# Attention layer 0 of a four-layer gated model: the softmax denominator split between GpSimd and the vector engine, and TensorE's filler products taken out

## The chip, the cores and the metric

The kernel runs on one NeuronCore of one Trainium2 chip. The core has TensorE (PE in the profile), the vector engine (DVE), the scalar engine (ACT), GpSimd (POOL) and SyncE (SP, which here only issues DMAs). The metric is the device time of one execution in microseconds (us); lower is better.

## The reference, cut to what matters

`x` is 16 batches of 256 rows of 128 numbers; the context has 64 rows a batch. Four layers follow each other, each a gated cross attention and a gated feed-forward. Only the attention of layer 0 is touched. Its softmax is unusual: it runs over the heads (axis 1), not over the keys.

```python
Q, K, V = query @ Wq.T + bq, key @ Wk.T + bk, value @ Wv.T + bv      # 16 heads of 8
energy = einsum('bhqd,bhkd->bhqk', Qh, Kh) / sqrt(8)
attn = softmax(energy, axis=1)                                       # over the 16 heads
out = einsum('bhqk,bhkd->bhqd', attn, Vh)
x = x + tanh(g_xattn[0]) * (out @ Wo.T + bo)
```

## The kernel before, in words

One program on five engines; each engine executes its own list in order, and semaphores hold the order between them. Each `Stage` field (`q.sub`, `q.esc`, `q.prob` and so on) is a semaphore with its base, and `q.sub(n)` means "n of these are done".

In attention layer 0 the 4096 rows of x are 32 tiles of 128 queries. A **unit** u is one tile; two units, an even one (qt = 0) and an odd one (qt = 1), are one batch b = u // 2, a **pair**. The scores of a unit are 128 partitions x 1024 numbers, ordered (head, key). They pass through these steps:

- PE `scores(b)` (L545) computes both units of a batch into the four banks of `psS`, at the end of even unit 2b - 4. It waits for DVE to have read the batch before (`q.sub(2 * b)`), for the queries, and for `kblk(b)`, the keys spread by head, which POOL writes in `keys` (L730).
- DVE `score_rows(u)` takes the maximum over heads (L672) and subtracts it into one of four slots of `sp`, a part of the tile `ring` (L676).
- ACT `exp_rows(u)` takes the exponential in place (L634).
- DVE `sum_rows(u)` adds up the 16 heads for each key (L688, read with a step of 64 numbers) and inverts the sum into `rden` (L690).
- POOL `scale(u)` multiplies the slot by the inverse, in place (L750). This is `prob(u)`.
- PE turns the slot in two halves h = 0, 1 of four 128 x 128 transposes (L554) through the one bank `psT`; ACT copies each half to `pT` (L638); PE multiplies by the values (L563) into `psO`; DVE copies the result (L694, `output`); PE projects it (L593) and adds the bias row (L594); DVE adds it to x (L699, `residual`); DVE then takes the statistics of the new rows for the next norm (L375).

The work is staggered. In its unit u an engine does:

- DVE: `score_rows(u+3)`, `output(u-1)`, `residual(u-2)`, `sum_rows(u+2)`, statistics of u-2.
- POOL: if u is even `keys(b+2)`, if u is odd `values(b+1)` (L739), then `scale(u+2)`.
- ACT: the copy of half 0; if u is even the queries, keys and values of batch b+2; the copy of half 1; `exp_rows(u+3)`.
- PE: transposes of u half 0; if u is even the projections of batch b+2 (L520 to L526); values of u-1, half 0; transposes of u half 1; values of u-1, half 1; projection of u-2; if u is even `scores(b+2)`.

PE also executes products that nothing reads (`keep_clock`, L533): four of the identity by itself ahead of each `scores` from batch 2 on, after the wait for `q.sub`, and three ahead of the first transposes of each unit from 1 on, after the wait for `q.pT`. Each such float32 product is two matmul records in the profile. The tile `late` is not in use in this stage, except that SP's zeroing DMAs read its part `zeros`, `late[:, 2 * CT:3 * CT]`.

Of the kernel before, what the change touches and what calls it, by code (L numbers as in the profile page):

```python
# [12 lines left out]
ALU = mybir.AluOpType  # L13
# [8 lines left out]
P = 128  # L22
B, S, SK, D = 16, 256, 64, 128
NH, DK = 16, 8
NT = B * S // P
CH = 4
NC = NT // CH
CT = CH * P
# [38 lines left out]
class Stage:  # L67


    def __init__(self, std=None, xn=None, xt=None, xnT=None, xs=None, kept=None, xa=None, ctx=None, kraw=None, vraw=None, kv=None, qp=None, qT=None, kblk=None, vblk=None, scores=None, mx=None, sub=None,  # L70
# [16 lines left out]
RN_STEPS = 13  # L87
LN_STEPS = dict(std=1, xn=NC, xa=NC, xt=NC, xnT=NC)
LN_PLACE = {0: 0, 1: 1}
ATT_STEPS = dict(kraw=B, vraw=B, kv=B, qp=B, qT=B, kblk=B, vblk=B, scores=B, mx=NT, sub=NT, esc=NT, esum=NT, erec=NT, prob=NT,  # L90
                 t=2 * NT, pT=2 * NT, o=NT, attnT=NT, y=NT, x=NT)
FFN_NAMES = "up act y x dup dact dy copied xgt xgT ye ix"

# [1 line left out]
def build(nc, ins, out, sorted_x, sorted_y):  # L95
    ctx = ExitStack()
    with ctx:
# [13 lines left out]
        ident = sb("ident", [P, P])  # L111
# [43 lines left out]
        kblk = sb("kblk", [P, 2, GH, SK])  # L155
        vblk = sb("vblk", [P, 2, NP, 4 * DK])
        ring = sb("ring", [P, NS, NH * SK])
        sbs, sp = ring[:, 0:2], ring[:, 2:6]
        pT = sb("pT", [P, 2, NP, P])
        mx = sb("mx", [P, 4, SK])  # L160
        kraw = sb("kraw", [P, 2, SK])
        vraw = sb("vraw", [P, 2, D])
# [7 lines left out]
        late = sb("late", [P, 5 * CT])  # L170
        xstage = late[:, 0:2 * CT].rearrange("p (s t d) -> p s t d", s=2, t=CH)
        zeros = late[:, 2 * CT:3 * CT]
        b2copy = late[:, 3 * CT:5 * CT].rearrange("p (s t d) -> p s t d", s=2, t=CH)
        wtn = b2copy[:, 0, 0:2]
        xg = sbs[:, 0, :].rearrange("p (s n) -> p s n", s=2)
# [16 lines left out]
        rows = sb("rows", [P, NT * 2], I32)  # L192
# [30 lines left out]
        psT = pb("psT")  # L223
# [288 lines left out]
        def known(k, low, high=NT + 2):  # L512

            return k is None or low <= k < high

        def att_tensor(pe, l):
            q = AT[l]

            def queries(b):
                nc.tensor.matmul(psM[:, 0:S], wat[:, l, 0, :], xnT[:, bass.ds(b * S, S)], start=True, stop=True).then_inc(q.qp.sem, 1)  # L520

            def keys_values(b, s):
                nc.tensor.matmul(psM[:, S:S + SK], wat[:, l, 1, :], ctxz[:, bass.ds(b * 2 * SK + SK, SK)], start=True, stop=True)
                for h in range(2):
                    at = S + SK + h * D // 2
                    mm = nc.tensor.matmul(psM[:, at:at + D // 2], ctxz[:, b * 2 * SK + (1 - h) * SK:b * 2 * SK + (3 - h) * SK],  # L526
                                          wat[:, l, 2, h * D // 2:(h + 1) * D // 2], start=True, stop=True)
                mm.then_inc(q.kv.sem, 1)

            def keep_clock(bank, count):  # L530

                for _ in range(count):
                    nc.tensor.matmul(bank, ident[:], ident[:], start=True, stop=True)  # L533

            def scores(b, s, first):
                if not first:
                    pe.wait_ge(*q.sub(2 * b))
                if not isinstance(b, int) or b > 1:
                    keep_clock(psS[:, 0, 0:P], 4)
                pe.wait_ge(*q.qT(b + 1))  # L540
                pe.wait_ge(*q.kblk(b + 1))
                for g in range(NG):
                    r = slice(32 * g, 32 * g + 32)
                    for qt in range(QT):
                        mm = nc.tensor.matmul(psS[:, g, qt * 256:qt * 256 + 256], qTs[r, s, qt * P:(qt + 1) * P],  # L545
                                              kblk[r, s, :, :].rearrange("p h k -> p (h k)"), start=True, stop=True)
                mm.then_inc(q.scores.sem, 1)

            def transpose_rows(u, j, h, first):
                if not first:  # L550
                    pe.wait_ge(*q.pT(2 * u + h))
                for i in range(4):
                    p = 4 * h + i
                    mm = nc.tensor.transpose(psT[:, i * P:(i + 1) * P], sp[:, j, p * P:(p + 1) * P], ident[:])  # L554
                mm.then_inc(q.t.sem, 1)

            def times_values(u, s, qt, h):

                pe.wait_ge(*q.pT(2 * u + h + 1))
                for g in (2 * h, 2 * h + 1):  # L560
                    for pp in range(2):
                        a = 2 * g + pp
                        mm = nc.tensor.matmul(psO[32 * g:32 * g + 32, qt, 0:P], vblk[:, s, a, :], pT[:, qt, a, :],  # L563
                                              start=(pp == 0), stop=(pp == 1), tile_position=(0, 32 * g))
                if h:
                    mm.then_inc(q.o.sem, 1)

            def unit(u, b, s, qt, k):
                j = 2 * s + qt
                last_s = s if qt else 1 - s  # L570
                if known(k, 1, NT):
                    pe.wait_ge(*q.pT(2 * u))
                    keep_clock(psT[:, 0:P], 3)
                if known(k, 0, NT):
                    pe.wait_ge(*q.prob(u + 1))
                    transpose_rows(u, j, 0, k == 0)
                if qt == 0 and known(k, 0, NT - 2 * QT):
                    pe.wait_ge(*q.vraw(b + 2))
                    pe.wait_ge(*q.qT(b + 2))
                    keys_values(b + 2, s)  # L580
                    queries(b + 2)
                if known(k, 1, NT + 1):
                    if known(k, 3):
                        pe.wait_ge(*q.x(u - 2))
                    pe.wait_ge(*q.vblk(b + qt))
                    times_values(u - 1, last_s, 1 - qt, 0)
                if known(k, 0, NT):
                    transpose_rows(u, j, 1, False)
                if known(k, 1, NT + 1):
                    times_values(u - 1, last_s, 1 - qt, 1)  # L590
                if known(k, 2):
                    pe.wait_ge(*q.attnT(u - 1))
                    nc.tensor.matmul(psO[:, qt, 256:256 + D], attnT[:, qt, :], wat[:, l, 3, :], start=True, stop=False)  # L593
                    nc.tensor.matmul(psO[:, qt, 256:256 + D], ones1[:, :], bo[:, l, :], start=False, stop=True).then_inc(q.y.sem, 1)  # L594
                if qt == 0 and known(k, 0, NT - 2 * QT):
                    scores(b + 2, s, False)

            def first_queries():
                pe.wait_ge(*LN[2 * l].xnT(1))
                pe.wait_ge(*q.vraw(2))  # L600
                queries(0)
                pe.wait_ge(*q.qT(1))
                queries(1)


            pe.wait_ge(s_vz, 1)
            if l == 0:
                pe.wait_ge(ld["attw"], 9 * 16)
            keys_values(0, 0)
            pe.wait_ge(*q.vraw(1))  # L610
            keys_values(1, 1)
            ln_tensor(pe, 2 * l, None, first_queries, lambda: scores(0, 0, True))
            pe.wait_ge(*LN[2 * l].xnT(NC))
            scores(1, 1, False)
            for k in range(NT + 2):
                unit(k, k // QT, k // QT % 2, k % QT, k)
# [48 lines left out]
        def att_vector(dve, l):  # L665
# [14 lines left out]

            def sum_rows(u, j, early):

                dve.wait_ge(*q.esc(u + 1))
                if not early:
                    dve.wait_ge(*q.prob(u - 1))
                rd = rden[:, j % 2, :]
                rows = sp[:, j, :].rearrange("p (h k) -> p k h", k=SK)
                nc.vector.tensor_reduce(rd, rows, AXX, ALU.add).then_inc(q.esum.sem, 1)  # L688
                dve.wait_ge(*q.esum(u + 1))
                nc.vector.reciprocal(rd, rd).then_inc(q.erec.sem, 1)  # L690
# [31 lines left out]
        def att_gpsimd(pool, l):  # L722
# [10 lines left out]
            def values(b, s, early):  # L733
# [8 lines left out]
                        bvh[:, :].rearrange("k (h g e d) -> k g h e d", h=2, g=NG, e=2)[:, :, :, pp, :], ALU.add)  # L742
                op.then_inc(q.vblk.sem, 1)

            def scale(u, j):

                buf = sp[:, j, :].rearrange("p (h k) -> p h k", k=SK)
                rd = rden[:, j % 2, :].rearrange("p (a k) -> p a k", a=1)
                pool.wait_ge(*q.erec(u + 1))
                nc.gpsimd.tensor_tensor(buf, buf, rd.broadcast_to([P, NH, SK]), ALU.mult).then_inc(q.prob.sem, 1)  # L750

            def unit(u, b, s, qt, k):
                j = 2 * s + qt
                if qt == 0 and known(k, 0, NT - 2 * QT):
                    keys(b + 2, s, False)
                if qt == 1 and known(k, 0, NT - QT):
                    values(b + 1, 1 - s, not known(k, 2))
                if known(k, 0, NT - 2):
                    scale(u + 2, (j + 2) % 4)

            for b in range(2):
                keys(b, b, True)
            values(0, 0, True)
            for v in range(1, 3):
                scale(v - 1, v - 1)
            units(pool, unit, 0)


# [1238 lines left out]
```

## Time and profile before

| | us |
|---|---|
| median of 3 runs | 1236.53 |
| lowest and highest | 1236.52, 1237.42 |
| the profiled execution | 1235.94 |
| its span in the profile | 1233.8 |
| attention layer 0 in it, first score reduce to last residual | 45.4 to 242.8 |

In rows of a timeline the first number is the start in us from the span's start, the second the duration; a bracket gives idle time just before the instruction and what ended it. Rows of groups give count, busy time, mean ns of one, and idle time before them. "PEclk" is the granted clock of TensorE as a share of its full 2.4 GHz, so that 0.50 is 1.2 GHz.

### The profile page before, as it was taken

The numbers are of one execution on the slowest core, as the hardware profiler recorded it, in microseconds if no ns is written. First come the engines' busy times: TensorE is split into PE (matmuls) and PEld (weight loads), VectorE is DVE, ScalarE is ACT, GpSimd is POOL, SyncE is SP. The second block draws the span as 40 slices with busy tenths as digits, with TensorE's granted clock in tenths as the row PEclk, the third lists the DMA queues.
The fourth block names the chain that finished last, engine by engine and source line by source line (L and its number), as shares of the span: only waits on it lengthen the run. The fifth ranks groups of instructions, "written<-read, shape, count | busy, mean of one in ns | idle before, by whom it ended". The sixth has DMA issues, their size and how long they took to land.

```text
span 1233.8 us, 25957 instructions
## 1 busy us (share of the span) xinstructions
PE 1022.7 (83%) x9008; PEld 827.8 (67%) x9008; DVE 783.6 (64%) x1696; ACT 633.9 (51%) x1462; POOL 611.6 (50%) x660
## 2 busy tenths in 40 slices
PE   1599999762999899994877989999999998739990
PEld 0477767552677899982556767677777776539990
DVE  2889899726204766863889978645545667746661
ACT  1544444331323566664665787666555656426660
POOL 0145554312777303708886776744454547465224
PEclk9899999955999899997999999999999999859995
DMA  8920000000111123311000000000050000013224
GB/s 247 286 63 1 1 1 1 1 0 9 48 64 52 53 75 88 108 46 31 20 21 8 2 1 2 2 2 1 2 154 1 1 2 2 1 54 93 83 71 111
DMA packets 75475, 55.80 MB, mean 45 GB/s; under 512 B 7411, under 2 KB 68467, under 8 KB 75252
## 3 DMA queue, kind: packets, MB, share of 16 engines
q1 hardware_dynamic: 69236, 41.92, 11.8%
q0 software_dynamic: 6144, 12.60, 3.4%
q8 instruction: 61, 1.00, 0.3%
q14 instruction: 34, 0.28, 0.1%
HBM read 32.48 MB, written 22.02 MB: 44 GB/s over the span
## 4 chain that ended last, share of the span: by engine, by line
PE 65%; DVE 15%; issue 7%; ACT 5%; POOL 4%; SPq 1%; DMA 1%; DVEq 1%; POOLq 0%; ACTq 0%
PE psS L1052 8%; PE psT L1499 6%; PE psO L1058 5%; PE psO L1563 5%; PE psS L1555 4%; PE psS L1488 3%; PE psO L1514 3%; PE psS L1058 3%; PE psO L981 3%; PE psS L973 3%; DVE rden L688 2%; POOL xrows L1210 2%; DVE x L1123 2%; PE psO L1521 2%; DVE ring L676 2%
## 5 line engine op out<-in xcount | busy, mean ns | idle before, releaser
L1828 POOL TENSOR_TENSOR ring<-ring,mx 128x1024 f32<-128x1024 f32 x96 | 182.2, 1905 | 121.3 <-DVE mx L1724 120.7
L1631 ACT ACTIVATE pT<-psT 128x512 f32<-128x512 f32 x192 | 114.4, 596 | 147.4 <-PE psT L1499 147.3
L1101 ACT ACTIVATE pT<-psS,b1copy 128x128 f32<-128x128 f32 x512 | 145.9, 368 | 84.7 <-PE psS L1052 84.6
L1210 POOL DMA_INDIRECT xrows<-sorted_y,rows x96 | 93.3, 971 | 184.9 <-DMA sorted_y<-pT 132.7
L1052 PE MATMUL psS<-ring 128*128 128x128 f32 x1024 | 138.7, 280 | 10.4 <-DVE ring L1141 9.7
L1716 DVE TENSOR_TENSOR ring<-psS,bias 128x1024 f32<-128x1024 f32 x96 | 113.0, 1219 | 44.6 <-PE psS L1488 44.1
L1499 PE MATMUL psT<-ident,ring 128*128 128x128 f32 x768 | 123.0, 284 | 17.0 <-ACT pT L1631 10.3
L1052 PEld LDWEIGHTS psS<-ring 128*128 128x128 f32 x1024 | 126.9, 195 | 12.5 <-DVE ring L1141 6.7
L750 POOL TENSOR_TENSOR ring<-ring,rden 128x1024 f32<-128x1024 f32 x32 | 75.4, 2355 | 115.3 <-DVE rden L690 115.3
L1499 PEld LDWEIGHTS psT<-ident,ring 128*128 128x128 f32 x768 | 86.8, 143 | 57.4 <-issue 34.5
L1724 DVE TENSOR_REDUCE mx<-ring 128x16 f32<-128x1024 f32 x96 | 112.1, 1209 | 0.0
L1138 DVE COPY ring<-w 128x512 f32 x128 | 59.8, 467 | 58.7 <-PE psO L1058 23.1
L1058 PE MATMUL psO<-ring,pT 128*128 128x128 f32 x640 | 86.0, 278 | 0.4 <-ACT pT L1101 0.3
L1058 PEld LDWEIGHTS psO<-ring,pT 128*128 128x128 f32 x640 | 79.1, 195 | 0.7 <-ACT pT L1101 0.7
L638 ACT ACTIVATE pT<-psT 128x512 f32<-128x512 f32 x64 | 38.2, 597 | 75.2 <-PE psT L554 75.2
L1243 POOL DMA_INDIRECT sorted_x<-late,ix x64 | 62.4, 975 | 23.4 <-issue 16.8
L1662 ACT ACTIVATE xn<-x,lnb,lnr 128x128 f32<-128x128 f32 x160 | 65.7, 492 | 11.8 <-POOL lnb L1849 11.8
L1769 DVE TENSOR_TENSOR x<-psO,x 128x512 f32<-128x512 f32 x16 | 11.1, 692 | 88.0 <-PE psO L1563 88.0
L688 DVE TENSOR_REDUCE rden<-ring 128x64 f32<-128x1024 f32 x32 | 61.4, 1919 | 0.0
L1563 PE MATMUL psO<-w,xrows 128*128 128x128 f32 x512 | 59.9, 276 | 0.3 <-ACT vblk L1653 0.3
L1563 PEld LDWEIGHTS psO<-w,xrows 128*128 128x128 f32 x512 | 58.4, 192 | 0.5 <-issue 0.5
L1007 ACT ACTIVATE ring<-psS,b 128x512 f32<-128x512 f32 x32 | 22.0, 687 | 69.4 <-PE psS L973 69.2
(273 smaller groups left out, 2251.9 us busy)
## 6 DMA issues: line engine op xcount, KB each, us to landing
w<-w_dram SPq DMA_DIRECT2D x34, 256.0 KB, 6.0
ring<-sorted_x SPq DMA_DIRECT2D x32, 256.0 KB, 2.9
sorted_y<-pT SPq DMA_DIRECT2D x32, 256.0 KB, 2.5
sorted_x<-late SPq DMA_DIRECT2D x20, 256.0 KB, 3.6
xrows<-sorted_y,rows POOLq DMA_INDIRECT x96
ctxz<-ctxz_dram SPq DMA_DIRECT2D x1, 1056.0 KB, 11.6
wat<-wat_dram SPq DMA_DIRECT2D x4, 256.0 KB
w<-w_dram SPq DMA_DIRECT2D x8, 128.0 KB, 2.6
```

Of the source, the lines that this page charges most:

```text
L688: nc.vector.tensor_reduce(rd, rows, AXX, ALU.add).then_inc(q.esum.sem, 1)
L750: nc.gpsimd.tensor_tensor(buf, buf, rd.broadcast_to([P, NH, SK]), ALU.mult).then_inc(q.prob.sem, 1)
L1052: mm = nc.tensor.matmul(psS[:, t % 2, f * P:(f + 1) * P], wcopy[:, t, 0, f, :], xgT[:, s, t * P:(t + 1) * P], start=True, stop=True)
L1058: mm = nc.tensor.matmul(moe_out[r][:, s, t * P:(t + 1) * P], hs[:, t % 2, f, :], wcopy[:, t, 1, f, :], start=(f == 0), stop=(f == nf - 1))
L1101: op = nc.scalar.activation(hs[:, t % 2, f, :], psS[:, t % 2, f * P:(f + 1) * P], func, bias=b1copy[:, t, f:f + 1])
L1210: nc.gpsimd.indirect_dma_start(fetched[:, at + m, :], None, sorted_y[c // (NC // 2)], bass.IndirectOffsetOnAxis(rows[:, c * nt + m:c * nt ...
L1499: mm = nc.tensor.transpose(psT[:, i * P:(i + 1) * P], ring[:, u % NS, p * P:(p + 1) * P], ident[:])
L1563: mm = nc.tensor.matmul(psB[:, t * P:(t + 1) * P], fourT[:, i % 2, k, t * P:(t + 1) * P], w22[:, e, f, :], start=(k == 0), stop=(k == 3))
L1631: nc.scalar.activation(pT[:, u % 2, 4 * h:4 * h + 4, :].rearrange("p a q -> p (a q)"), psT[:, :], ACT.Exp).then_inc(s_pT, 1)
L1716: nc.vector.tensor_tensor(ring[:, u % NS, :].rearrange("p (g h k) -> p g h k", g=NG, h=GH), psS[:, :, qt * 256:(qt + 1) * 256].rearrange(" ...
L1724: nc.vector.tensor_reduce(mx[:, u % 4, 0:NH], ring[:, u % NS, :].rearrange("p (h k) -> p h k", k=SK), AXX, ALU.max).then_inc(s_max, 1)
L1828: nc.gpsimd.tensor_tensor(rows_, rows_, mx[:, u % 4, 0:NH].rearrange("p h -> p h ()").broadcast_to([P, NH, SK]), ALU.subtract).then_inc(s_ ...
```

## The change

`late[:, 0:2 * CT]` gets a second name, `hsum`, with two slots of 512 numbers. POOL's new `add_halves(u)` waits for the exponentials of u and adds heads 8 to 15 of the slot to heads 0 to 7 into `hsum` (128 x 512). DVE's `sum_rows(u)` waits for that (`q.added`) in place of the exponentials and reduces 8 partial sums for each key in place of 16. In POOL's unit u `add_halves(u+3)` stands after `scale(u+2)`. `keep_clock` and both calls of it go.

```diff
+        hsum = late[:, 0:2 * CT].rearrange("p (s n) -> p s n", s=2)
...
-            def keep_clock(bank, count):
-
-                for _ in range(count):
-                    nc.tensor.matmul(bank, ident[:], ident[:], start=True, stop=True)
-
             def scores(b, s, first):
                 if not first:
                     pe.wait_ge(*q.sub(2 * b))
-                if not isinstance(b, int) or b > 1:
-                    keep_clock(psS[:, 0, 0:P], 4)
...
                 if known(k, 1, NT):
                     pe.wait_ge(*q.pT(2 * u))
-                    keep_clock(psT[:, 0:P], 3)
...
             def sum_rows(u, j, early):
 
-                dve.wait_ge(*q.esc(u + 1))
+                dve.wait_ge(*q.added(u + 1))
...
-                rows = sp[:, j, :].rearrange("p (h k) -> p k h", k=SK)
+                rows = hsum[:, j % 2, :].rearrange("p (h k) -> p k h", k=SK)
...
+            def add_halves(u, j, early):
+
+                pool.wait_ge(*q.esc(u + 1))
+                if not early:
+                    pool.wait_ge(*q.esum(u - 1))
+                half = NH * SK // 2
+                nc.gpsimd.tensor_tensor(hsum[:, j % 2, :], sp[:, j, 0:half], sp[:, j, half:], ALU.add).then_inc(q.added.sem, 1)
+
...
                 if known(k, 0, NT - 2):
                     scale(u + 2, (j + 2) % 4)
+                if known(k, 0, NT - 3):
+                    add_halves(u + 3, (j + 3) % 4, False)
...
-            for v in range(1, 3):
-                scale(v - 1, v - 1)
+            add_halves(0, 0, True)
+            add_halves(1, 1, True)
+            scale(0, 0)
+            add_halves(2, 2, False)
+            scale(1, 1)
             units(pool, unit, 0)
```

## Rows read from the trace of the kernel before

**Rows 1.** Stretches of 10 us: PE, PEld, DVE, ACT, POOL busy, then PEclk, DMA

```profile
50.00:60.00 10.00, 6.36 (x33) 4.94 (x33) 9.86 (x10) 4.27 (x8) 4.79 (x3) 0.50 1.03 295
...
100.00:110.00 10.00, 9.30 (x83) 7.04 (x83) 9.06 (x12) 4.71 (x8) 4.66 (x5) 1.00 0.01 2
```

**Rows 2.** DVE's timeline over one pair and a little more

```profile
108.03 1.91 DVE L688 TENSOR_REDUCE rden<-ring 128x64 f32<-128x1024 f32 x1
...
109.98 0.55 DVE L690 RECIPROCAL rden<-rden 128x64 f32<-128x64 f32 x1
...
110.60 1.20 DVE L672 TENSOR_REDUCE mx<-psS 128x64 f32<-128x1024 f32 x1
...
111.94 1.23 DVE L676 TENSOR_TENSOR ring<-psS,mx 128x1024 f32<-128x1024 f32 x1
...
114.16 0.35 DVE L699 SCALAR_TENSOR_TENSOR x<-psO,tg,x 128x128 f32 x1 [0.63 <-PE psO L594]
...
114.43 1.93 DVE L688 TENSOR_REDUCE rden<-ring 128x64 f32<-128x1024 f32 x1
...
119.95 1.92 DVE L688 TENSOR_REDUCE rden<-ring 128x64 f32<-128x1024 f32 x1
```

**Rows 3.** The timeline of PE, ACT and POOL over the same pair

```profile
107.72 1.16 PE L533 MATMUL psS<-ident 128*128 128x128 f32 x8 [0.65 <-DVE ring L676]
...
108.81 1.17 PE L545 MATMUL psS<-kblk,qTs 32*128 32x256 f32 x16
...
109.90 0.94 PE L533 MATMUL psT<-ident 128*128 128x128 f32 x6
...
110.61 2.37 POOL L750 TENSOR_TENSOR ring<-ring,rden 128x1024 f32<-128x1024 f32 x1 [2.47 <-DVE rden L690]
...
110.67 0.60 PE L554 MATMUL psT<-ident,ring 128*128 128x128 f32 x4
...
113.53 0.48 PE L594 MATMUL psO<-bo,ones 1*128 1x128 f32 x2
...
114.72 0.60 PE L554 MATMUL psT<-ident,ring 128*128 128x128 f32 x4
...
118.49 0.48 PE L594 MATMUL psO<-bo,ones 1*128 1x128 f32 x2
```

**Rows 4.** Groups by line, operation and shape, whole span

```profile
L750 POOL TENSOR_TENSOR ring<-ring,rden 128x1024 f32<-128x1024 f32 x32 | 75.4, 2355 | 115.3 <-DVE rden L690 115.3
...
L1855 POOL TENSOR_TENSOR x<-x,bx 128x512 f32<-128x512 f32 x24 | 30.5, 1270 | 0.0
...
L1828 POOL TENSOR_TENSOR ring<-ring,mx 128x1024 f32<-128x1024 f32 x96 | 182.2, 1905 | 121.3 <-DVE mx L1724 120.7
...
L730 POOL TENSOR_TENSOR kblk<-kraw,hmask 128x256 f32<-128x256 f32 x16 | 11.6, 725 | 24.5 <-ACT kraw L627 24.5
...
L1724 DVE TENSOR_REDUCE mx<-ring 128x16 f32<-128x1024 f32 x96 | 112.1, 1209 | 0.0
```

**Rows 5.** PE's timeline in a later stage, at its longer idle times

```profile
603.41 0.66 PE L1499 MATMUL psT<-ident,ring 128*128 128x128 f32 x4 [2.02 <-POOL ring L1828]
...
612.22 0.69 PE L1514 MATMUL psO<-pT,late 128*32 128x128 f32 x16 [2.60 <-DVE vraw L1733]
...
612.85 2.09 PE L1488 MATMUL psS<-xnT,qTs 32*128 32x256 f32 x16
...
614.87 1.11 PE L1499 MATMUL psT<-ident,ring 128*128 128x128 f32 x4
```

**Rows 6.** Stretches of 2 us of that stage: PE busy, PEclk, DMA

```profile
612.00:614.00 2.00, 1.78 (x28) 0.67 0.00 0
...
616.00:618.00 2.00, 2.00 (x26) 0.98 0.13 33
```

**Rows 7.** DVE's sums at the two ends of the stage

```profile
72.33 1.92 DVE L688 TENSOR_REDUCE rden<-ring 128x64 f32<-128x1024 f32 x1
...
227.04 1.92 DVE L688 TENSOR_REDUCE rden<-ring 128x64 f32<-128x1024 f32 x1
```

More of the change, by code:

```diff
@@ L89 @@
 LN_PLACE = {0: 0, 1: 1}
-ATT_STEPS = dict(kraw=B, vraw=B, kv=B, qp=B, qT=B, kblk=B, vblk=B, scores=B, mx=NT, sub=NT, esc=NT, esum=NT, erec=NT, prob=NT,
+ATT_STEPS = dict(kraw=B, vraw=B, kv=B, qp=B, qT=B, kblk=B, vblk=B, scores=B, mx=NT, sub=NT, esc=NT, added=NT, esum=NT, erec=NT, prob=NT,
                  t=2 * NT, pT=2 * NT, o=NT, attnT=NT, y=NT, x=NT)
```

## The prediction

> **What bounds the kernel now.** I read the stretches of 10 us first. While attention layer 0 is in full swing, DVE is busy for 9.06 of 10 us and PE for 9.30, GpSimd for 4.66 and ACT for 4.71, at full clock; the stage starts at half clock, 0.50 [rows 1]. Two engines look full, so the shares don't decide. PE's share is partly the products that nothing reads: in one pair 8 records ahead of `scores` and 6 ahead of each unit's first transposes [rows 3].
>
> Second, DVE's timeline. I measure by the starts of its sums, two for a pair: 108.03 (in an even unit), 114.43 (odd), 119.95 (even) [rows 2]. So the even half of a pair lasts 6.40 us, the odd half 5.52, a pair 11.92. In the odd half DVE never idles: sum, reciprocal, maximum and subtraction alone take 1.92 + 0.55 + 1.20 + 1.23 = 4.90 us of 5.52 and the rest are the small copies. In the even half it idles 0.63 us ahead of the residual, released by PE's bias product [rows 2].
>
> Third, what PE did until then. Released by DVE's subtraction at 107.72, it ran the products that nothing reads (1.09 us to the next start), the scores (1.09), products again (0.77), then from the first transposes at 110.67 to the bias product at 113.53, which ends 0.48 later [rows 3]. So in the even half the path is DVE subtraction, PE, DVE residual, and 1.86 us of it is filler. In the odd half it is DVE. GpSimd waits 2.47 us for the reciprocal before its scale [rows 3] and bounds nothing.
>
> **The change, part by part.** In what follows 0 is the start of the sum in an even unit, u + 2.
>
> *The sum of half the numbers.* The trace has no reduce of 512 strided numbers. The strided one of 1024 takes 1.92 us [rows 2]; a contiguous one of 1024 takes 1.21 [rows 4]. From below 0.60, half of the contiguous one; from above 1.13, half of 1.92 plus half of the 0.35 that 128 numbers cost at L699 [rows 2], as if all of that were a fixed part. I take 1.04, near the upper end, since the step of 64 numbers stays. To the start of the reciprocal that is 1.07. The Trainium skill (VectorE: DVE Perf Modes, The perf-mode tier table) has every `tensor_reduce` at one element a cycle, which would give an estimate of 0.69 for 512; our row of 1.92 for 1024 contradicts it for this access, and by 0.69 a pair would be 0.35 shorter.
>
> *GpSimd's new addition*, 128 x 512, two inputs. L1855 is an addition of that size: 1.27 us [rows 4]. Below: 0.95, half of L1828 (1.905); above: 1.35, half of L750 (2.355) plus the 0.17 that I allow for a fixed part. I take 1.27. The Trainium skill (GPSIMD Reference, Engine selection) speaks against this edit: elementwise work of two inputs belongs on VectorE, GpSimd being about twice as slow. In busy time it is right here: 1.27 us are bought to save 0.88 on DVE. But GpSimd had 2.47 us idle, so what counts is whether it lies in a loop.
>
> *It does lie in one, and that is the new wait.* GpSimd's order is scale(u+2), addition(u+3); DVE's is sum(u+3), reciprocal. The sum waits for the addition, the addition is queued behind the scale, the scale waits for the reciprocal before. One turn: sum 1.07, reciprocal to scale 0.63 (109.98 to 110.61), scale 2.35, addition 1.27, handoff 0.08 (as from the reciprocal's end at 110.53 to 110.61) [rows 2 to 4]. Sum: **5.40 us**. DVE alone would need 5.52 - 0.88 = 4.64, so it now waits some 0.7 us ahead of the sum; behind the waiting sum stand the reciprocal, the statistics and the next maximum. The odd half is 5.40 instead of 5.52: of DVE's 0.88, only 0.12 is left.
>
> *The keys are pushed back too.* `keys(b+2)` is queued behind addition(u+2), so it starts at -0.08, takes 0.73 [rows 4], and PE's `scores(b+2)` can't start before 0.71, though DVE freed the bank about a microsecond earlier. From there: scores 1.09, first transposes to residual 3.49 (110.67 to 114.16), residual to sum 0.27 [rows 2, 3]; no filler. Even half: 0.71 + 1.09 + 3.49 + 0.27 = **5.56 us** (GpSimd's loop would allow 5.40), against 6.40. The scores end at about 1.9, DVE wants them at 1.69, a wait of 0.3 that this path hides.
>
> A pair is then 5.40 + 5.56 = **10.96 us** against 11.92. From the sum at 72.33 to the one at 227.04 are 13 pairs [rows 7], 154.7 us; 13 x 10.96 = 142.5. That is 12.2 us less. At the start the extra work of GpSimd and the lost filler meet the cold clock in both versions; I count nothing, with 3 us either way. At the end the last scale waits for one more turn of 5.40 where DVE did it in 3.6; filler ahead of the last transposes goes; 0.3 us more. So far **-11.9 us**.
>
> *What the filler hid.* Without it PE has, in my schedule, this in each pair: scores at 0.71, odd unit's transposes at 1.80, its bias product at 4.66, even unit's transposes at 5.08 (0.42 behind it; the scale that they need ended at 4.05), end of its bias product 4.25 later (114.72 to 118.97) at 9.33 [rows 3]. Then it is idle until the scores at 10.96 + 0.71 = 11.67: **2.34 us**, once a pair, where it had 0.65. The trace shows what such gaps do. In the later attention stage PE idled 2.02 us until 603.41 and kept the full clock; it idled 2.60 us until 612.22 and then had half clock (0.67 on average from 612 to 614), with full clock again from about 616 [rows 5, 6]. They are the nearest below and above; 2.34 is in the middle. Half clock cost there 2.09 us for scores that take 1.17 at full clock [rows 3] and 1.11 for transposes that take 0.66: 0.92 + 0.45 = 1.37 us, and in the even half the scores and transposes are on the path. I take the clock to fall in 6 of the 13 pairs: 6 x 1.37 = 8.2 us. It can't stay low: PE's 8.3 us of work in a pair would be over 14 at half clock, more than the pair, so PE would be busy throughout, as it was in the stretch ahead of the rise at 616 [rows 6].
>
> Sum: -11.9 + 8.2 = **-3.7 us**. The profiled execution took 1235.94 (span 1233.8 and 2.1 around it), the median of the runs is 1236.53, 0.6 more; -3.7 from the median is 1232.8.
>
> **The rivals.**
>
> *The clock holds* in all pairs. For it: the gap of 2.02 was harmless, and if the true sum or addition is cheaper the gap shrinks with it. Then all of the 11.9 stays: 1236.5 - 11.9 = 1224.6.
>
> *The clock falls in every pair*, the other side. Place: the scores and transposes behind the 2.34 us gap. Price 1.37 x 13 = 17.8, less 11.9: 5.9 us slower, 1242.4; and more where a fall lasts longer than there. It decides from 8.7 falls on (11.9 / 1.37). For it: the gap of 2.60 cost the clock, and every shift that makes GpSimd later widens the gap. Against it: the gap comes at the same place of each pair, but the odds that I read from two rows are even, not certain.
>
> *The shorter sum isn't shorter*, so that the change doesn't do what it says: if the 1.92 came from something other than the count, the odd half is 5.40 + 0.88 = 6.28, the even one still 5.56 (DVE has room there), a pair 11.84. That saves 1 us, and the gap grows to 3.2, longer than the one that cost the clock: 1236.5 - 1 + 17.8 = 1253. Against it: a contiguous reduce of the same 1024 numbers takes 1.21, so most of it goes by the elements.
>
> *The sum and addition are cheaper than I take* (0.60 and 0.95): the odd half would be 4.6 to 4.7, a pair near 10.2, the gap 1.6, no falls: 13 x 1.7 = 22 us, 1214. Both at their lower ends is unlikely.
>
> **How the numbers follow.** Falls on some pairs, 1232.8 with 1228 to 1238 around it: 0.42. Clock holds: 0.26. Falls in every pair: 0.22. Sum not shorter, or another wait: 0.06. Both prices at their ends: 0.04. For 8 in 10 the range runs from 1222 (clock holds, and a little of the start) to 1244 (falls everywhere, one or two of them long). A measurement of this kernel tells a change from none at about 0.2%, 2.5 us. Faster by more: 0.28 of the first case, 0.25, 0.04, together 0.57 and 0.02 of the rest: 0.59. Within: 0.12 of the first, 0.05 of the others: 0.17. Slower: 0.24.
>
> **What the profile of the changed kernel would show.** Sums of half the size near 1.04 us, additions near 1.27; DVE idle ahead of the sum, released by GpSimd, about 0.7 us in odd halves; PE idle ahead of the scores near 2.3 us once a pair, released by GpSimd's keys; sums 5.56 and 5.40 us apart in pairs at full clock, and half clock in some of the pairs. If PEclk is 1.00 from 70 us to 240, the forecast is too high by 8. If pairs are longer than 11.9 it is too low. It would be wrong otherwise if the addition slowed ACT or DVE beside it, or if the later stages' clock falls at other places because all of them come earlier.

## The result, and the profile after

| | before | after |
|---|---|---|
| median, us | 1236.53 (4 runs) | 1259.16 (4 runs) |
| lowest and highest | 1235.46, 1237.42 | 1252.46, 1262.70 |
| the profiled execution, and its span | 1235.94, 1233.8 | 1262.70, 1260.9 |
| mean granted clock in it | 0.927 | 0.884 |
| attention layer 0, last residual ends at | 242.8 | 265.3 |

The change makes the kernel slower: ratio 1.0172, 95% interval 1.0148 to 1.0195, 22.6 us in the medians. That is above the forecast of 1232.8 and above its range of 1222 to 1244. In the profiled executions, of which that of after is the slowest of its four, the spans differ by 27.1 us. Of these, 22.5 lie in the stage that was edited: its last residual ends that much later. What follows took 995.6 us against 991.0. That part has no edit in any kernel here and took 989.5 to 995.0 in the first group of runs below, so I don't put its 4.6 us down to the change.

I read the page of after first: busy time by engine, and the granted clock in 40 slices.

```profile
PE 1031.6 (82%) x8710; PEld 822.5 (65%) x8710; DVE 756.4 (60%) x1696; ACT 634.2 (50%) x1462; POOL 652.5 (52%) x692
...
PEclk9787777755699899998899999999999999868995
```

The clock shows 7 and 8 in the slices from 60 to 250 us. In stretches of 10 us, the same columns as [rows 1], the full clock of before is gone there:

```profile
100.00:110.00 10.00, 9.35 (x68) 6.32 (x64) 7.31 (x11) 4.38 (x9) 5.84 (x6) 0.79 0.00 1
110.00:120.00 10.00, 8.38 (x55) 5.96 (x56) 5.82 (x9) 3.60 (x5) 5.61 (x6) 0.66 0.01 2
120.00:130.00 10.00, 7.72 (x57) 5.09 (x57) 7.83 (x12) 3.10 (x6) 8.11 (x7) 0.74 0.00 0
```

DVE, busy for 9.06 of 10 us in [rows 1], is down to 5.82 to 7.83: it has less to do and waits more. Now one pair in the timeline (start, duration, engine; the bracket is idle time and what ended it), to be set beside [rows 2, 3]:

```profile
123.16 1.27 POOL L744 TENSOR_TENSOR late<-ring 128x512 f32<-128x512 f32 x1
124.39 0.72 POOL L723 TENSOR_TENSOR kblk<-kraw,hmask 128x256 f32<-128x256 f32 x1
124.46 1.03 DVE L681 TENSOR_REDUCE rden<-late 128x64 f32<-128x512 f32 x1 [0.60 <-POOL late L744]
125.25 2.11 PE L539 MATMUL psS<-kblk,qTs 32*128 32x256 f32 x16 [2.28 <-POOL kblk L723]
126.15 2.35 POOL L751 TENSOR_TENSOR ring<-ring,rden 128x1024 f32<-128x1024 f32 x1 [1.04 <-DVE rden L683]
127.30 1.11 PE L548 MATMUL psT<-ident,ring 128*128 128x128 f32 x4
128.34 1.08 PE L557 MATMUL psO<-pT,vblk 128*32 128x128 f32 x8
129.35 1.12 PE L548 MATMUL psT<-ident,ring 128*128 128x128 f32 x4
130.39 1.08 PE L557 MATMUL psO<-pT,vblk 128*32 128x128 f32 x8
132.52 0.35 DVE L692 SCALAR_TENSOR_TENSOR x<-psO,tg,x 128x128 f32 x1 [0.70 <-PE psO L587]
132.79 1.02 DVE L681 TENSOR_REDUCE rden<-late 128x64 f32<-128x512 f32 x1
138.18 1.03 DVE L681 TENSOR_REDUCE rden<-late 128x64 f32<-128x512 f32 x1 [0.69 <-POOL late L744]
```

The order is the forecast one: addition (L744), then keys (L723), then PE's scores (L539) after an idle 2.28 us that the keys end. But everything PE then does takes the time of half clock: scores 2.11 us, transposes 1.11, values products 1.08, transposes 1.12, values products 1.08. The sums are at 124.46, 132.79 and 138.18: the even half lasts 8.33 us where 5.56 was forecast, the odd half 5.39 (5.40 forecast). PE and PEclk in stretches of 2 us around that gap:

```profile
122.00:124.00 2.00, 0.98 (x8) 1.00 0.00 0
124.00:126.00 2.00, 0.75 (x8) 0.69 0.00 0
126.00:128.00 2.00, 2.00 (x20) 0.50 0.00 0
128.00:130.00 2.00, 2.00 (x13) 0.50 0.00 0
130.00:132.00 2.00, 2.00 (x14) 0.60 0.00 0
132.00:134.00 2.00, 2.00 (x15) 1.00 0.00 0
```

The 0.69 from 124 to 126 puts the fall to 1.2 GHz at 124.76, half a microsecond before the gap ends; the 0.60 from 130 to 132 puts the rise at about 131.6. So 6.8 us at half clock, and the stretch from 132 on is at 2.4 GHz again.

I placed every fall in this way, from stretches of 1 us. Between the sum of tile 4 (72.61) and that of tile 30 (247.32) the clock falls 13 times, once in each pair. The first two low spells last 3.4 us, and their even halves 7.00 and 6.91; the other eleven last 6.8 us (one fall every 13.65 us) and go with even halves of 8.23 to 8.34. In this pattern pair and clock fit each other: an even half of 8.3 with an odd one of 5.35 is a pair of 13.65 us, just the distance between two falls, so each pair meets the fall at the same place. Behind these pairs, in the stage's tail, the clock falls once more, at 247.63 us, and stays low for 13.65 us. In before it holds to the end of the stage, until 244.0. The tail of after, same columns as above:

```profile
248.00:261.00 13.00, 12.88 (x68) 8.25 (x67) 4.38 (x11) 3.17 (x6) 6.47 (x5) 0.50 0.00 1
```

The groups of the edited lines, whole span:

```profile
L744 POOL TENSOR_TENSOR late<-ring 128x512 f32<-128x512 f32 x32 | 40.7, 1271 | 24.4 <-ACT ring L627 24.4
L681 DVE TENSOR_REDUCE rden<-late 128x64 f32<-128x512 f32 x32 | 32.9, 1029 | 10.6 <-POOL late L744 10.6
L539 PE MATMUL psS<-kblk,qTs 32*128 32x256 f32 x256 | 31.9, 632 | 35.0 <-POOL kblk L723 30.8 <-issue 4.2
```

Addition 1271 ns and sum 1029 ns are the prices of the forecast (1.27 and 1.04). The scores waited 30.8 us in all for the keys.

### The profile page after: what moved, and what is told of

It reads as the page before. It is cut to its first block, busy times and chain, and to the rows that moved or that the text cites. A ratio compares the mean times of both kernels' runs of the same rounds, so it can differ in the third digit from the quotient of the medians.

```text
span 1260.9 us, 25429 instructions
## 1 busy us (share of the span) xinstructions
PE 1031.6 (82%) x8710; PEld 822.5 (65%) x8710; DVE 756.4 (60%) x1696; ACT 634.2 (50%) x1462; POOL 652.5 (52%) x692
## 4 chain that ended last, share of the span: by engine, by line
PE 60%; issue 15%; DVE 9%; POOL 8%; ACT 4%; SPq 1%; DMA 1%; DVEq 1%; POOLq 0%; ACTq 0%
PE psS L1058 9%; PE psT L1505 6%; PE psO L1064 5%; PE psO L1569 5%; PE psS L1561 4%; PE psO L1520 3%; PE psS L1494 3%; PE psS L1064 3%; PE psO L987 3%; POOL late L744 3%; PE psS L979 3%; DVE x L1129 2%; POOL xrows L1216 2%; PE psO L1527 2%; PE psO L1460 2%
## 5 line engine op out<-in xcount | busy, mean ns | idle before, releaser
L1834 POOL TENSOR_TENSOR ring<-ring,mx 128x1024 f32<-128x1024 f32 x96 | 182.4, 1907 | 120.0 <-DVE mx L1730 119.5
L1505 PE MATMUL psT<-ident,ring 128*128 128x128 f32 x768 | 124.8, 286 | 19.4 <-ACT pT L1637 11.9
L1668 ACT ACTIVATE xn<-x,lnb,lnr 128x128 f32<-128x128 f32 x160 | 65.8, 494 | 13.8 <-POOL lnb L1855 13.8
L548 PE MATMUL psT<-ident,ring 128*128 128x128 f32 x256 | 57.2, 363 | 4.4 <-POOL ring L751 2.6
L539 PE MATMUL psS<-kblk,qTs 32*128 32x256 f32 x256 | 31.9, 632 | 35.0 <-POOL kblk L723 30.8
```

Source lines behind the costliest of these rows:

```text
L1505: mm = nc.tensor.transpose(psT[:, i * P:(i + 1) * P], ring[:, u % NS, p * P:(p + 1) * P], ident[:])
L1668: op = nc.scalar.activation(to[:, t, :], x[:, c * CH + t, :], ACT.Identity, bias=lnb[:, k, t:t + 1], scale=lnr[:, k, t:t + 1])
L1834: nc.gpsimd.tensor_tensor(rows_, rows_, mx[:, u % 4, 0:NH].rearrange("p h -> p h ()").broadcast_to([P, NH, SK]), ALU.subtract).then_inc(s_ ...
```

## The experiments

Each edit is against the kernel after, if nothing else is said. "Falls" are falls of the clock in the 13 pairs between the sums of tiles 4 and 30; "idle" is PE's idle time from the end of a pair's other work to its scores. Each ratio is to before, from runs on the same chip (kernels of one group share them). The "tail" runs from the sum of tile 30 to the end of the last residual.

### First group: which part of the change costs the time (before: 1238.07)

**e1, both sets of filler products back**, so that only the split of the sum is left.

```diff
+                if not isinstance(b, int) or b > 1:
+                    keep_clock(psS[:, 0, 0:P], 4)
...
                     pe.wait_ge(*q.pT(2 * u))
+                    keep_clock(psT[:, 0:P], 3)
```

> The changed kernel with both sets of filler products back, so that only the split of the sum is left. Clock theory (the loss comes from half clock behind a 2.3 us gap of PE in each pair): the gap is filled to under 1.3 us, PEclk is 1.00 from 70 to 240 us, the even half is 5.56 + 0.77 of filler ahead of the transposes = 6.33, the odd half 5.40, a pair 11.73 against 11.92 of before: about 1234, 2.5 below before. Wait theory (the addition in GpSimd's loop and the late keys are themselves what costs): pairs stay at 13 us or more, 1250 to 1260.

1234.88 us, ratio 0.9966 [0.9953, 0.9979]. Even halves 6.33 to 6.43, odd ones 5.32 to 5.43, no fall, as expected. The split by itself gains 3.2 us: the odd half goes by GpSimd's loop and the even half by PE with its fillers, as the forecast's own terms have it.

**e2, before without its filler products**: the other half of the change alone.

```diff
-                if not isinstance(b, int) or b > 1:
-                    keep_clock(psS[:, 0, 0:P], 4)
...
-                    keep_clock(psT[:, 0:P], 3)
```

> The kernel before with both sets of filler products taken out and nothing else. Clock theory: at full clock the pair would be DVE's own 11.3 us, PE has 8.3 us of work in it and so a gap near 2.7 ahead of the scores, longer than the 2.6 that cost the clock; half clock then adds to the even half what it added in the changed kernel (2.8) less the 1.2 that DVE has in hand: pairs near 12.9, 1245 to 1250. Wait theory: nothing waits longer and 1.86 us of filler leave the path in each pair, DVE's idle 0.63 goes: 13 x 0.63 = 8 us faster, 1228.

1240.95 us, ratio 1.0027 [1.0007, 1.0047]. The idle ahead of the scores is 1.54 and 1.83 us in the first two pairs; there the clock holds and the even halves are 5.42 and 5.51, so the filler really was on PE's path. Behind them the idle is 1.91 to 1.96, and from 95.6 us on the clock falls, 11 times. Nine of the low spells last 3.4 us, with even halves of 6.44 to 6.57; the two of 6.8 us go with 7.8. Around the gap that ends at 118.07:

```profile
116.00:118.00 2.00, 0.15 (x2) 1.00 0.00 0
118.00:120.00 2.00, 1.93 (x22) 0.87 0.00 0
120.00:122.00 2.00, 2.00 (x13) 0.50 0.00 0
122.00:124.00 2.00, 2.00 (x15) 0.78 0.00 0
```

The clock is still full when the scores start and falls at 119.5, behind them. The place of the fall matters little here: the one at 129.7, inside the gap that ends at 130.05, goes with an even half of 6.56, this one with 6.48. A short spell costs 1.0 to 1.1 us here and 1.4 in e3 and e7. A likely reason, argued and not tested, is that the scores start 0.25 us behind DVE's sum here (118.07 and 117.82) and 0.79 behind it in after, so PE has some time in hand. 1240.95 is below the 1245 to 1250 expected. The miss is the price: I had given every fall the 2.8 us of after's long spells, less 1.2.

**e3, only the four products ahead of the scores back.** The first two added lines of e1.

> The changed kernel with only the four filler products ahead of the scores back. They stand in the gap and off the path. Clock theory: gap pieces of 0.7 and 0.6 us, PEclk 1.00, pair 5.56 + 5.40 = 10.96, 1224.6 and so 12 below before. Wait theory: as the changed kernel, 1250 to 1260.

1227.96 us, ratio 0.9899 [0.9865, 0.9933]. The idle is 0.48 ahead of the products and 0.65 behind them. Even halves 5.62 to 5.71, and 7.02 to 7.09 in three pairs: there the clock fell, which I had not expected. The saving is 10.1 us where 12 was expected.

**e4, only the three products ahead of the transposes back.** The last added line of e1.

> The changed kernel with only the three filler products ahead of each unit's first transposes back. Clock theory: they delay PE by 0.77 in the odd unit and 0.77 in the even one, so that the gap ahead of the scores is 2.34 - 0.77 = 1.57 us, shorter than the 2.02 that kept the clock; PEclk 1.00, even half 6.33, odd 5.40, pair 11.73, 1234 to 1235. Wait theory: 1250 to 1260.

1249.86 us, ratio 1.0080 [1.0053, 1.0108]. A miss: I expected the clock to hold. The gap is 1.56 to 1.57 us, below the 2.02 that had been harmless in [rows 5] (1.25 and 1.47 in the first two pairs), and the clock fell 9 times, for 3.4 us each. PE's scores in one pair, and PE with PEclk around them:

```profile
124.08 1.48 PE L544 MATMUL psS<-kblk,qTs 32*128 32x256 f32 x16 [1.57 <-POOL kblk L729]
```

```profile
122.00:124.00 2.00, 0.51 (x3) 1.00 0.00 0
124.00:126.00 2.00, 1.92 (x18) 0.70 0.00 0
126.00:128.00 2.00, 2.00 (x12) 0.50 0.03 8
```

So in these pairs filler products as such don't keep the clock; those in the gap keep it better. e3 and e4 differ in where the products stand, and by 21.9 us. Not all of that is the clock: the three products ahead of the transposes are also on PE's path, and even halves without a fall are 6.33 to 6.43 here and 5.62 to 5.71 in e3, some 9 us in 13 pairs.

### Second group: the size of the gap, and GpSimd's loop (before: 1341.86)

In this group the whole program, before included, took some 100 us more, outside this stage; so I compare within the group and by the halves of the pairs, which were as in the first group. A ratio here stands for about 8% more us than in the other groups.

**e5, six products ahead of the scores.** As e3, with 6 for 4.

> The changed kernel with six filler products ahead of the scores, where the run with four still lost the clock in 3 pairs. Six take 1.65 us of the 2.28 that PE has to wait for the keys and end when the keys do. Clock theory: no or one fall from 70 to 240 us, pairs of 11.05 as in the full-clock pairs with four, 2 to 4 us below the run with four, about 1225. Rival (the falls with four were no matter of idle time, but came of themselves): again 3 or 4 falls, the same time as with four.

1328.02 us, ratio 0.9912 [0.9886, 0.9939]. PE and GpSimd in one pair:

```profile
124.68 1.60 PE L534 MATMUL psS<-ident 128*128 128x128 f32 x12 [0.48 <-DVE ring L676]
125.62 0.73 POOL L730 TENSOR_TENSOR kblk<-kraw,hmask 128x256 f32<-128x256 f32 x1
125.78 1.03 DVE L688 TENSOR_REDUCE rden<-late 128x64 f32<-128x512 f32 x1 [0.70 <-POOL late L751]
126.50 1.17 PE L546 MATMUL psS<-kblk,qTs 32*128 32x256 f32 x16 [0.21 <-POOL kblk L730]
127.60 0.66 PE L555 MATMUL psT<-ident,ring 128*128 128x128 f32 x4
```

The products, 1.60 us of them, end before the keys do and cost nothing: the scores still wait 0.21 for the keys, then take 1.17, not 2.11. No fall in the pairs; even halves 5.62 to 5.72, odd ones 5.32 to 5.43, a pair 11.04. It is 13.8 us below before in the medians. This is the forecast's schedule at full clock (5.56, 5.40, 10.96), and it is 2.6 us a pair shorter than after, with the same work and six products more.

**e6, three small products more, ahead of the wait for the subtraction.**

```diff
+                if not isinstance(b, int) or b > 1:
+                    pe.wait_ge(*q.vraw(b + 1))
+                    for _ in range(3):
+                        nc.tensor.matmul(psM[:, S + SK + D:512], ident[:], ident[:, 0:64], start=True, stop=True)
                 if not first:
                     pe.wait_ge(*q.sub(2 * b))
+                if not isinstance(b, int) or b > 1:
+                    keep_clock(psS[:, 0, 0:P], 6)
```

> As the one with six, and three more products of 64 columns ahead of the wait for the subtraction, in the other piece of the gap (about 0.7 us), into a part of a bank that nothing reads. Clock theory: idle time of PE under 0.5 us a pair, no falls; 1224.6, the time of the rival in which the clock holds. If they make PE late for the scores, the even halves grow by up to 0.3: then 1226 to 1229.

1329.83 us, ratio 0.9916 [0.9893, 0.9940]. The same halves as e5, but for a first even one of 5.87, and no fall. PE idles for less than 0.1 us at a time ahead of the scores; against the 0.48 and 0.21 of e5 that gains nothing more.

**e7, two products ahead of the scores.**

> The changed kernel with two filler products ahead of the scores. PE idles 1.7 us a pair in pieces of 0.7 and 1.1 us, where 2.28 lost the clock in each pair, 1.57 in one piece in 10 of 14, and 1.2 in two pieces in 3. Clock theory (idle time in all counts): falls in 6 to 10 pairs, 1238 to 1248. Rival (only the longest single gap counts): a longest gap of 1.1 is as with four, 2 to 4 falls, 1228.

1337.34 us, ratio 0.9976 [0.9957, 0.9995]. Idle 0.48 and 1.10. Seven falls, each with 3.4 us of half clock, the last of them behind the last scores; even halves 5.62 to 5.71 without one and 6.95 to 7.10 with one, so a fall costs 1.4 us. The count fits "idle time in all" (6 to 10 expected) and not the rival (2 to 4). But the longest single piece also grew, from 0.65 in e3 to 1.10, so a rule by the longest piece is not excluded. The time, 4.5 us below before, is better than the 1238 to 1248 expected. One of the falls:

```profile
118.05 1.33 PE L546 MATMUL psS<-kblk,qTs 32*128 32x256 f32 x16 [1.10 <-POOL kblk L730]
119.31 1.11 PE L555 MATMUL psT<-ident,ring 128*128 128x128 f32 x4
```

```profile
118.00:120.00 2.00, 1.95 (x19) 0.73 0.00 0
120.00:122.00 2.00, 2.00 (x13) 0.50 0.00 0
122.00:124.00 2.00, 2.00 (x17) 0.91 0.00 0
```

**e8, both fillers, no addition**: the sum reads heads 0 to 7 alone, and heads 8 to 15 are left out of the denominator.

```diff
-                dve.wait_ge(*q.added(u + 1))
+                dve.wait_ge(*q.esc(u + 1))
...
-                rows = hsum[:, j % 2, :].rearrange("p (h k) -> p k h", k=SK)
+                rows = sp[:, j, 0:NH * SK // 2].rearrange("p (h k) -> p k h", k=SK)
...
-                    add_halves(u + 3, (j + 3) % 4, False)
```

> Both sets of filler products as before, DVE sums only heads 0 to 7 and heads 8 to 15 are left out of the denominator, GpSimd adds nothing. Against the run with both fillers it takes GpSimd's addition out of the loop and lets the keys go early. Theory (the addition took back DVE's 0.88): the odd half is 5.52 - 0.88 = 4.64, but the even half stays at 6.40 since its path runs through PE, and PE with its fillers has 11.3 us of work in a pair: pairs of 11.3, 1229 to 1230. Rival (DVE's sum is not what set the odd half): 1234, as with the addition.

1329.91 us, ratio 0.9926 [0.9900, 0.9951]. Sums in DVE's timeline:

```profile
118.39 1.03 DVE L689 TENSOR_REDUCE rden<-ring 128x64 f32<-128x512 f32 x1
...
124.62 1.03 DVE L689 TENSOR_REDUCE rden<-ring 128x64 f32<-128x512 f32 x1
...
129.33 0.35 DVE L700 SCALAR_TENSOR_TENSOR x<-psO,tg,x 128x128 f32 x1 [0.26 <-PE psO L595]
129.60 1.03 DVE L689 TENSOR_REDUCE rden<-ring 128x64 f32<-128x512 f32 x1
```

Even half 6.23, odd half 4.98. With the same fillers e1 has 6.33 to 6.43 and 5.32 to 5.43, so GpSimd's addition costs 0.35 to 0.45 in the odd half: that is the loop. An odd half of 4.64 was expected, DVE's own time. It is longer because DVE now waits 0.26 us for PE's bias product in the odd half too. The even half hardly moves (6.20 to 6.30, where 6.40 was expected); PE has it.

### Third group: the keys off GpSimd (before: 1238.32)

**e9, the vector engine spreads the keys, four products ahead of the scores.** GpSimd's `keys` for batches 2 on goes to DVE, ahead of its sum.

```diff
+            def keys(b, s):
+
+                dve.wait_ge(*q.kraw(b + 1))
+                dve.wait_ge(*q.scores(b - 1))
+                nc.vector.tensor_tensor(kblk[:, s, :, :], kraw[:, s, :].rearrange("p (a k) -> p a k", a=1).broadcast_to([P, GH, SK]),
+                                        hmask[:, :, :], ALU.mult).then_inc(q.kblk.sem, 1)
...
                     residual(u - 2, qt)
+                if qt == 0 and known(k, 0, NT - 2 * QT):
+                    keys(b + 2, s)
...
-                if qt == 0 and known(k, 0, NT - 2 * QT):
-                    keys(b + 2, s, False)
```

> The changed kernel with four filler products ahead of the scores, and the spreading of the keys by head moved from GpSimd to the vector engine, ahead of its wait for the sum, where it idles 0.6 us in each pair. Theory (with the clock held, the even half of 5.66 us is keys, scores and PE's products, and the odd half of 5.37 is GpSimd's loop): the scores start 0.8 us earlier, both halves are GpSimd's loop, 5.36, a pair 10.72 against 11.05: 3 to 5 us below the run with six products, 16 below before. Rival (the even half is set by something else): pairs of 11.05 as there, 12 to 14 below before.

1223.88 us, ratio 0.9885 [0.9863, 0.9908]: 14.4 us below before, the lowest ratio of all (16 below was expected; its interval meets those of e3, e5 and e11). Three engines in one pair:

```profile
119.99 1.05 DVE L688 TENSOR_REDUCE rden<-late 128x64 f32<-128x512 f32 x1
124.01 1.27 POOL L760 TENSOR_TENSOR late<-ring 128x512 f32<-128x512 f32 x1
124.32 1.16 PE L534 MATMUL psS<-ident 128*128 128x128 f32 x8 [0.67 <-DVE ring L676]
124.64 0.93 DVE L696 TENSOR_TENSOR kblk<-kraw,hmask 128x256 f32<-128x256 f32 x1
125.49 1.02 DVE L688 TENSOR_REDUCE rden<-late 128x64 f32<-128x512 f32 x1
125.72 1.17 PE L546 MATMUL psS<-kblk,qTs 32*128 32x256 f32 x16 [0.24 <-DVE kblk L696]
130.88 1.04 DVE L688 TENSOR_REDUCE rden<-late 128x64 f32<-128x512 f32 x1 [0.17 <-POOL late L760]
```

Idle 0.67 and 0.24. The even half is 5.39 (125.49 to 130.88), now GpSimd's loop, which ends DVE's wait of 0.17; the odd half is 5.50 and DVE's again, since the spread takes 0.93 us there, more than the wait of 0.6 that it was to fill: a pair is 10.83, not the 10.72 expected. Full clock until 211 us, behind the last scores.

**e10, the same with no filler at all.**

> As the one before, without any filler products. Clock theory: PE still has only 8.3 us of work in a pair of 10.7, a gap near 2.1 us ahead of the scores, and loses the clock in each pair; the early keys leave PE's path 0.7 us in hand, so a fall costs 0.7 (if it lasts 3.4 us) to 2.0 (6.8 us): between 6 below and 10 above before. Rival (the late keys were the harm, not the missing products): pairs of 10.7, 15 below before.

1240.52 us, ratio 1.0023 [1.0006, 1.0040]. The gap is 1.68 and 1.77 us in the first two pairs and 1.87 to 1.89 in the others, ended by DVE's keys. The clock falls 13 times, 11 of them for 3.4 us, with even halves of 6.31 to 6.54, and two for 6.8 us, with 7.7 and 7.8. One gap and the scores behind it:

```profile
121.92 2.11 PE L539 MATMUL psS<-kblk,qTs 32*128 32x256 f32 x16 [1.87 <-DVE kblk L689]
```

The same schedule as e9's but for the four products and the clock, and 16.6 us longer.

**e11, the same with six products.**

> Vector engine's keys with six filler products. Theory: six end 0.55 us later than four and push the scores back by that, PE's path is then as long as GpSimd's loop, 5.4; no falls at all, where four may leave one or two: the same time as with four within 3 us.

1226.18 us, ratio 0.9904 [0.9882, 0.9925]. Halves as in e9: four are enough. Its tail takes 19.9 us and e9's 17.3.

**e12, before with only its four products ahead of the scores.**

```diff
                     pe.wait_ge(*q.pT(2 * u))
-                    keep_clock(psT[:, 0:P], 3)
```

> The kernel before with only the four products ahead of the scores; the three ahead of each unit's transposes are out. Clock theory: at full clock the pair would be DVE's own 11.3 us; PE's gap ahead of the subtraction is 1.9 us, as in the run without any, and it loses the clock in most pairs, at a cost of about 1 us each which the shorter path gives back: within 3 us of before. Rival: 8 us below before.

1239.48 us, ratio 1.0013 [0.9999, 1.0027]. Even halves 5.63 to 5.68 at full clock, 7.01 to 7.24 in six pairs with a fall. The gap is 0.68 and 1.27 us in the first two pairs and 1.35 to 1.38 in the others, not the 1.9 expected, and lies ahead of the products. So in before the three products do keep the clock, by ending PE's work later, and what they cost and what they save is about the same.

### All of them by the idle time

| PE idle ahead of the scores, us a pair, from the third pair on | kernel | falls in the 13 pairs |
|---|---|---|
| 0.1 or less | e6, e8 | 0 |
| 0.48 to 0.50 | e1 | 0 |
| 0.54 to 0.63 | e11 | 1, in the last, behind the last scores |
| 0.65 | before | 0 |
| 0.48 + 0.21 | e5 | 0 |
| 0.66 to 0.75 + 0.24 | e9 | 1, in the last, behind the last scores |
| 0.48 + 0.65 | e3 | 3 |
| 1.36 | e12 | 6 |
| 0.48 + 1.10 | e7 | 7, the last behind the last scores |
| 1.57 | e4 | 9 |
| 1.88 | e10 | 13 |
| 1.93 | e2 | 11 |
| 2.28 | after | 13 |

The table is about the pairs alone. In the tail, where there are no more scores, the three products ahead of the transposes go with the clock: before, e1, e4 and e8, which have them, keep it full until the last residual or a microsecond before it, and their tails take 15.1 to 16.0 us. All ten kernels without them lose it there; their tails take 16.0 to 19.9, with 17.9 in after and 18.0 in e5. No run puts these products back in the tail alone.

## Why the prediction was wrong, point by point

**The sum and the addition**: right. 1.03 and 1.27 us. The estimate of 0.69 by the Trainium skill (VectorE: DVE Perf Modes, The perf-mode tier table) would have been wrong, as the row of 1.92 for 1024 numbers said.

**GpSimd's loop**: right. Odd halves are 5.31 to 5.40 against 5.40, with DVE idle for 0.60 to 0.69 us (0.7 forecast) and released by the addition. e8 shows the cause: without the addition, 4.98, where DVE waits for PE in part.

**The keys pushed back, and the pair at full clock**: right. The scores wait for the keys, and start 0.72 us behind the sum in e5 (0.71 forecast, though its two stated terms, -0.08 and 0.73, give only 0.65). e5 has 5.62 to 5.72 and 5.32 to 5.43, a pair 11.04 for 10.96. Had that been all, e5's 13 pairs (143.5 us) against the 154.7 of before is 11.2 us less (12.2 forecast). Its tail gives back 2.3 us of that.

**The gap**: right in place and size, 2.28 us for 2.34.

**What the gap does**: this is the step that failed, "I take the clock to fall in 6 of the 13 pairs: 6 x 1.37 = 8.2 us". The number is 13, not 6. The price of 1.37 was taken from a fall that hits the scores and the first transposes alone. For a low spell of 3.4 us it holds: 1.3 in after's first two pairs, 1.4 in e3 and e7, and between 1.0 and 1.7 in the other runs. But from the third pair on each low spell lasts 6.8 us and also slows both values products (1.08 us for 0.64) and the transposes of the second half (1.12 for 0.66), all on the path. By the even halves, the first two pairs lose 6.96 - 5.67 = 1.3 us each, the other eleven 8.30 - 5.67 = 2.6. The sum made again: 143.5 + 2 x 1.3 + 11 x 2.6 = 174.7 us, and the trace has 174.7 from the sum at 72.61 to that at 247.32. Against 154.7 that is +20.0; the stage starts 0.3 later and its tail, 15.7 us before, takes 17.9 (0.3 forecast, 2.2 measured). Together +22.5 at the last residual. The 0.3 itself is what e1 and e4 show, whose tails run at full clock: 16.0. That after lost the other 1.9 to the fall at 247.63, which the forecast left out, is argued, not shown, since e1 and e4 also differ from it by the products ahead of the transposes.

**Why I took 6**: I read the two gaps of [rows 5] as a scale on which 2.02 us was safe and 2.60 not, and 2.34 half way. For that stage the scale is borne out: two more of its gaps, 1.98 until 624.53 and 2.87 until 633.61, kept the clock and lost it, in this order. e12 and e4 show that this scale doesn't carry over: here 1.36 us already costs the clock in 6 pairs and 1.57 in 9. What PE does around the gap differs between the stages; which part of it matters was not tried.

**The rivals**: the second, the clock falls in every pair, came true, with its own clause that a fall may last longer than there. With its count and its price of 1.37 it gave 1242.4, 17 us below what was measured: the long spells are most of that. The clock held in all 13 pairs only where products fill the gap (e5, e6) or both sets are back (e1). The sum was shorter, and neither price was at its lower end, so the other two rivals are out. That the fillers, and not the split, carry the loss is shown by e1 (both back, 3.2 us faster than before) and by e5 (six products in the gap, 0.9912). That the work itself did not slow, but PE's clock, is shown by e9 against e10: same lists but for four products, which nothing reads, and 16.6 us. The mean durations of DVE's, ACT's and GpSimd's instructions, kind by kind, agree within 0.01 us between the two.

**What stays open**: why a low spell lasts 3.4 us in some pairs and 6.8 in others. After, e2 and e10 have both; e3, e4, e7 and e12 have only the short ones among their pairs. Open too is which gap costs the clock in which pair: the falls get more frequent with the idle time, but at nearly the same idle time e4 has 9 falls and e7 has 7, e10 has 13 and e2 has 11.

## What to carry to other kernels

A matmul that nothing reads is not free to remove because nothing reads it: look at the idle time that it stands in and ask what the granted clock does once it is gone, and put it where PE waits anyway, where it costs nothing (e5: 1.60 us of products, scores still waiting 0.21). When a clock fall is priced from another stage, price all work that stands on the path in a whole low spell, and don't take a gap that was harmless elsewhere for a safe one. When work is moved onto an engine with room, count what is queued behind it there: GpSimd's 1.27 us left 0.1 to 0.2 of DVE's 0.88 in the odd half, and the keys behind it made the gap.

## What the runs showed of the hardware that I had not expected

- Idle times of 1.36 to 1.57 us, once in a pair of 11 to 13 us, lost the full clock in about half to two thirds of the pairs, while a single one of 2.02 kept it in another stage [rows 5]. Split in two around four products (0.48 + 0.65) they still lost it three times.
- The clock and the loop can lock: in after, falls and pairs both come every 13.65 us, with 6.8 us at 1.2 GHz in each. There a gap of 2.28 us costs 2.6 us a pair more than the same gap filled (e5).
- A fall is not always at the gap. In e2 one comes 1.4 us behind its end (119.5 and 118.07), and the pair loses 1.0 us all the same.
- The spread of the keys, 128 x 256 with two inputs in SBUF, takes 0.96 us in the mean on DVE (14 of them, e9) and 0.725 on GpSimd. The Trainium skill (GPSIMD Engine Reference, Engine selection) has GpSimd about twice as slow for two inputs; the row goes the other way here, for the reason that follows. In e9 it starts at 124.64, beside GpSimd's addition, which reads SBUF until 125.28. The Trainium skill (SBUF — State Buffer, Who interferes with whom) says that a DVE instruction with two inputs in SBUF contends with a GpSimd instruction that reads it. The traces agree, and show its size: in each of the 14 spreads of e9, as in those of e10 and e11, the spread ends 0.28 or 0.29 us after the GpSimd instruction beside it, whether they overlap for 0.64 or 0.96 us. That is as if DVE did its work only once GpSimd was done. So the 0.96 is mostly waiting; on DVE with GpSimd idle the spread was never timed. The longest:

```profile
69.81 1.27 POOL L760 TENSOR_TENSOR late<-ring 128x512 f32<-128x512 f32 x1
70.13 1.24 DVE L696 TENSOR_TENSOR kblk<-kraw,hmask 128x256 f32<-128x256 f32 x1
```
